# Cached values fetched page by page by SP, GpSimd's splits moved, x kept by samples, half of it and the tokens stored later

## The reference

```
x = x + L0(x)   # gated MLP, 1376 wide: down(silu(gate(x)) * up(x)), each with adapters
x = x + L1(x)   # linear 512 -> 512 with bias and adapters
x = x + L2(x)   # the same, other weights
x = x + L3(x)   # attention over a paged cache
# L3, per sample: 32 query heads and 8 key heads of size 128, page size 32, 16 pages
q, k, v = x @ Wq.T, x @ Wk.T, x @ Wv.T
q, k = rope(rmsnorm(q, wq), pos), rope(rmsnorm(k, wk), pos)   # pos = seqlen + arange(128)
k_all, v_all = concat(k_cache[block_table], k), concat(v_cache[block_table], v)  # 512 cached + 128 new
scores = q @ k_all.T / sqrt(128); cached keys at or past seqlen are masked with -1e30
o = softmax(scores) @ v_all;  L3(x) = o @ Wo.T
```

## Time and profile before

| | |
|---|---|
| median of 3 runs | 1463.56 us |
| profiled execution | 1464.6 us |
| its span | 1462.9 us |
| TensorE busy | 1371.6 us, 94% of the span |
| VectorE, ScalarE, GpSimd busy | 77%, 57%, 43% |

### The profile page before, as it was taken

The page is one execution under the profiler, slowest core; times in us unless marked ns, Lnnn a source line. Parts: engine busy times, 40 slices in busy tenths (PEclk is TensorE's granted clock), DMA queues, the critical chain, the costliest instruction groups (busy, mean ns, idle before and its releaser), DMA issues.

```text
span 1462.9 us, 26792 instructions
## 1 busy us (share of the span) xinstructions
PE 1371.6 (94%) x7308; PEld 1161.9 (79%) x7308; DVE 1127.4 (77%) x2945; ACT 838.2 (57%) x1951; POOL 631.5 (43%) x726
## 2 busy tenths in 40 slices
PE   6999999937999999789999998899999989999996
PEld 5888888726888888678888887788888877888885
DVE  5532446738888889788888888788888888888885
ACT  5632333237555667565666676566666765665564
POOL 4000000027444446674445468545554685444441
PEclk9999999968999999999999999999999999999999
DMA  8111300193322243332222443222224332222211
GB/s 303 50 58 44 108 24 26 63 328 86 78 62 59 57 115 88 93 79 59 57 57 57 122 107 86 58 64 66 66 63 120 96 95 64 65 74 61 57 30 14
DMA packets 127314, 119.30 MB, mean 82 GB/s; under 512 B 84128, under 2 KB 94752, under 8 KB 127008
## 3 DMA queue, kind: packets, MB, share of 16 engines
q0 software_dynamic: 19936, 57.69, 15.2%
q1 hardware_dynamic: 106608, 60.51, 14.6%
q10 hardware_dynamic: 720, 0.54, 0.1%
HBM read 101.90 MB, written 16.78 MB: 81 GB/s over the span
## 4 chain that ended last, share of the span: by engine, by line
PE 60%; DVE 7%; issue 6%; POOL 3%; ACT 2%; DMA 1%; DVEq 0%; POOLq 0%; ACTq 0%
PE bank L1335 14%; PE tail L1374 13%; PE wide L1404 12%; PE tail L1451 11%; PE wide L1369 6%; PE bank L1356 3%; POOL wqT L1201 2%; DVE ra L1655 1%; DVE prT L1664 1%; DVE ra L1659 1%; DVE rb L1656 1%; ACT pr L1525 1%; DMA rope<-rope_tables 1%; PE tail L1426 1%; POOL wkvT L1201 1%
## 5 line engine op out<-in xcount | busy, mean ns | idle before, releaser
L1525 ACT ACTIVATE pr<-pr,nm,q_scale 128x640 f32<-128x640 f32 x256 | 235.7, 921 | 111.7 <-DVE nm L1689 110.5
L1374 PE MATMUL tail<-prT,vt 128*128 128x512 f32 x960 | 259.9, 412 | 24.3 <-DVE prT L1664 24.3
L1166 POOL TENSOR_TENSOR tick<-tick 128x1 f32<-128x1 f32 x191 | 58.9, 308 | 419.6 <-PE wide L1404 345.6
L1374 PEld LDWEIGHTS tail<-prT,vt 128*128 128x128 f32 x960 | 174.3, 193 | 67.5 <-DVE prT L1664 35.1
L1685 DVE CUSTOM_DVE_ANT_0 pr<-wide,bias 128x640 f32<-128x640 f32 x256 | 209.8, 819 | 14.4 <-issue 14.2
L1335 PE MATMUL bank<-wqT,xTb 128*128 128x512 f32 x768 | 206.3, 397 | 1.3 <-POOL wqT L1201 1.3
L1451 PE MATMUL tail<-woT,oT 128*128 128x512 f32 x768 | 195.9, 398 | 0.0
L1664 DVE TENSOR_TENSOR prT<-wide,prT 128x1024 fp32r<-128x1024 f32 x128 | 153.5, 1220 | 24.4 <-ACT prT L1517 22.3
L1404 PE MATMUL wide<-kT,qT 128*128 128x320 f32 x512 | 162.7, 318 | 7.7 <-DVE mx L1685 7.7
L1451 PEld LDWEIGHTS tail<-woT,oT 128*128 128x128 f32 x768 | 139.6, 188 | 26.8
L1404 PE MATMUL wide<-kT_low,qT 128*128 128x320 f32 x512 | 158.6, 310 | 0.0
(11 more groups left out here) (239 smaller groups left out, 2669.3 us busy)
## 6 DMA issues: line engine op xcount, KB each, us to landing
w_ring<-pair_weights SPq DMA_DIRECT2D x80, 256.0 KB, 3.6
xTb<-x_transposed POOLq DMA_DIRECT2D x32, 512.0 KB, 3.9
k_raw<-k_pages SPq DMA_DIRECT2D x512, 32.0 KB, 1.8
rope<-rope_tables POOLq DMA_DIRECT2D x32, 256.0 KB
out<-y POOLq DMA_DIRECT2D x32, 256.0 KB, 4.1
w_raw<-w_gate_up SPq DMA_DIRECT2D x10, 512.0 KB, 3.2
x_transposed<-xh SPq DMA_DIRECT2D x8, 512.0 KB, 6.5
w_raw<-w_down SPq DMA_DIRECT2D x11, 256.0 KB, 2.9
```

Of the source, the lines that this page charges most:

```text
L1166: nc.gpsimd.tensor_tensor(tick[:, 2:3], tick[:, 1:2], tick[:, 1:2], ALU.add).then_inc(s_carry, 1)
L1374: last = nc.tensor.matmul(tail[g][:, :], vt[:, v_part, j, g * D:(g + 1) * D], prT[:, p_part, j, :], start=(j == 0 and v_part + p_part == 0 ...
L1525: ac.activation(pr[:, h, :], pr[:, h, :], ACT.Exp, bias=nm[:, h:h + 1], scale=q_scale[:, 0, head(h)], accum_out=den[:, h:h + 1]).then_inc( ...
```

## The change

- The values are laid out in DRAM by page and pair, and SP loads them with 16 DMAs per unit as it does the keys. The row numbers, their making in the first block and the four gathers are gone. SP also loads the rope table of each unit, once the unit before has been rotated.
- GpSimd's key split waits in addition for the first six normalisations of the unit before; its value split for both rotations and for the sums of the unit before, no longer for the first score. `add_share` comes after the value split and adds the share of the unit just before.
- In the last unit of a pair GpSimd makes chunks 0 to 2 before the value split and 3 to 11 after it (before 0 to 7 and 8 to 11), from VectorE's third step on. In the first unit it makes all eight output chunks after the value split (before four and four). ScalarE's copies stand earlier to match.
- `mask_keys` stands first in VectorE's turn.
- `xh` is laid out by sample, so that a sample is one run of 4096 bytes per partition. The first block stores only samples 0 to 3 of it. Samples 4 to 7 and the tokens are stored by GpSimd in the attention block, whose first action is the load of the first x. SP now waits in the first block until its four stores have landed.
- SP's order at the start of attention: 8 weight chunks, rope, 4 chunks, keys, values, 4 chunks (before: 12 chunks, keys, 4 chunks).
- The tensors in SBUF are placed in another order, so that what is still being stored isn't overwritten.

The diff, cut to its core:

```diff
@@ first block, SP @@
-                for c in range(2):
-                    sp.wait_ge(s_xl, 2 * 2 * KT + (c + 1) * KT)
-                    for i in range(c * BLK, (c + 1) * BLK):
-                        sp.dma_start(x_scratch[i].rearrange("p (t c) -> p t c", t=2 * KT),
-                                     xh[:, :, :, i * S:(i + 1) * S].rearrange("p i k c -> p (i k) c").bitcast(F32)).then_inc(s_xs, 16)
-                    for i in range(c * BLK, (c + 1) * BLK):
-                        sp.wait_ge(m_free[i % 2], i // 2 + 1)
-                        sp.dma_start(out[i], x_tok[:, i, :]).then_inc(s_init, 16)
+                sp.wait_ge(s_xl, 5 * KT)
+                for i in range(BLK):
+                    sp.dma_start(x_scratch[i], flat(xh[:, i], "i k c").bitcast(F32)).then_inc(s_xs[0], 16)
                 sp.wait_ge(s_ropest, 16)
+                sp.wait_ge(s_xs[0], 16 * BLK)
...
@@ attention @@
-    EARLY = {"next": ((0, 1, 2, 3), (4, 5), (6,), (7,)), "out": ((), (12, 13), (14,), (15,)), None: ((), (), (), ())}
+    EARLY = {"next": ((0,), (1, 2, 3), (4, 5, 6, 7), (8,), (9,), (10,)), "out": ((), (), (), (12, 13), (14,), (15,)), None: ((),) * 6}
...
+            load_x(0)
...
+            for i in range(BLK, B):
+                nc.gpsimd.dma_start(x_scratch[i], xh[:, i].rearrange("p i k c -> p (i k c)").bitcast(F32)).then_inc(s_xs[1], 16)
...
+            def split_keys(u, n):
                 pool.wait_ge(s_k, u * (16 * NPP) + 16 * NPP)
                 pool.wait_ge(s_sfull, u * HP + HP)
+                pool.wait_ge(s_p[0], u * SOON + FIRST)
...
+            def split_values(u, n):
+                pool.wait_ge(s_vnew, u + 1)
+                pool.wait_ge(s_v, u * (16 * NPP) + 16 * NPP)
+                pool.wait_ge(s_pv, u * G + FIRST)
+                pool.wait_ge(s_rope, u * G + 2 + FIRST)
...
+            def turn(pair, b, n, share, then_x, stored, extra=None):
+                u = unit(pair, b)
+                split_keys(u, n)
                 if then_x is not None:
                     pool.wait_ge(s_q1, u + 1)
                     carry(n + 1)
                     load_x(then_x)
                     n = n + 1
+                if share is None:
+                    for i in range(B):
+                        nc.gpsimd.dma_start(out[i], x_tok[:, i, :]).then_inc(s_init, 16)
+                share_room(u, stored)
+                if extra == "next":
+                    pool.wait_ge(s_step, u * NSTEP + 3)
+                    low_weights(pair + 1, 0, 3)
+                split_values(u, n + 1)
+                if share is not None:
+                    add_share(u - 1, share, n + 2)
+                else:
+                    pool.wait_ge(s_init, 16 * B)
                 if extra:
+                    low_weights(chunk_pair(pair, extra), *((3, 3 * KT) if extra == "next" else (3 * KT, NCHUNK)))
...
+            def load_rope(pair, b):
+                sp.wait_ge(s_rope, unit(pair, b) * G + FIRST)
+                sp.dma_start(rope[:, :, :].rearrange("p i d -> p (i d)"),
+                             rope_scratch[bass.ds(b, 1)].rearrange("o p n -> (o p) n")).then_inc(s_ropel, 16)
+
+            def load_values(pair, b, pages):
+                sp.wait_ge(s_vs, unit(pair, b) + FIRST)
+                for j, page in enumerate(pages):
+                    i = j % (P // PSIZE)
+                    sp.dma_start(v_raw[i * PSIZE:(i + 1) * PSIZE, j // (P // PSIZE), :],
+                                 v_pages[bass.ds(page * NPAIR + pair, 1)].rearrange("o s n -> (o s) n")).then_inc(s_v, 16)
...
@@ SP, per pair @@
+                load_weights(pair, 4 * KT, NCHUNK)
+                load_unit(1, pair, 1)
                 with sp.Fori(0, B - 2) as b:
+                    load_unit(2, pair, b + 2)
                 load_weights(pair + 1, 0, 2 * KT)
+                pages = pages_of(3, 0)
+                load_weights(pair + 1, 2 * KT, 2 * KT + 3)
+                load_keys(pair + 1, 0, pages)
+                load_rope(pair + 1, 0)
+                load_weights(pair + 1, 2 * KT + 3, 4 * KT)
+                load_values(pair + 1, 0, pages)
...
@@ VectorE's turn @@
                 if front:
+                    mask_keys()
                     arrive()
                     v.tensor_copy(qk[:, 0:REP, :], bank[1][:, :].rearrange("p (h d) -> p h d", d=D)).then_inc(s_q0, 1)
```

More of the change, by code:

```diff
@@ L231, in build_program @@
         s_xl = sem("x_updated_low_part")
-        s_xs = sem("x_stored")
+        s_xs = [sem(f"x_stored{c}") for c in range(2)]
         s_tok = sem("x_tokens_ready")
@@ L386, in main @@
                         for w_part, x_part in PASSES:
-                            last = nc.tensor.matmul(gate_up_place(j, c, w), wT[:, j % 2, w, w_part, k, :], xh[:, x_part, k, half(c)],
+                            last = nc.tensor.matmul(gate_up_place(j, c, w), wT[:, j % 2, w, w_part, k, :], x_half(x_part, k, c),
                                                     start=(k == 0 and w_part + x_part == 0), stop=False)
@@ L399, in lora_a @@
                                 out = wide[c][:, (2 * w + q) * 2 * S:(2 * w + q + 1) * 2 * S]
-                                tokens = slice(pair * 2 * S, (pair + 1) * 2 * S)
+                                two = slice(2 * pair, 2 * pair + 2)
                                 a_part = a_hl[:, w * KT:(w + 1) * KT, pair].rearrange("p k t m -> p k (t m)")
@@ new lines, in _ @@
+            turn(0, 0, 0, None, 1, False, "out")
+            pool.wait_ge(s_xs[1], 16 * BLK)
+            turn(0, 1, 3, 0, 2, False)
+            BEGUN = 3 + CARRIES
+            with pool.Fori(0, NPAIR - 1) as pair:
+                with pool.Fori(0, B - 3) as b:
+                    turn(pair, b + 2, pair * NCARRY + b * CARRIES + BEGUN, b + 1, b + 3, True)
+                turn(pair, B - 1, pair * NCARRY + (BEGUN + CARRIES * (B - 3)), B - 2, 0, True, "next")
+                turn(pair + 1, 0, pair * NCARRY + (BEGUN + CARRIES * (B - 2)), B - 1, 1, True, "out")
+                turn(pair + 1, 1, pair * NCARRY + (BEGUN + CARRIES * (B - 1)), 0, 2, True)
@@ L1273, in _, with pages_of @@
+            turn(pair, B - 1, pair * NCARRY + (BEGUN + CARRIES * (B - 3)), B - 2, None, True)
+            pool.wait_ge(s_out, 16 * (NPAIR * B - 1))
+            nc.gpsimd.memset(tick[:, 3:4], 0.0).then_inc(s_added, 1)
+            add_share(NPAIR * B - 1, B - 1, pair * NCARRY + (BEGUN + CARRIES * (B - 2) - 1))
+            pool.wait_ge(s_out, 16 * (NPAIR * B))
         @block.sync
         def _(sp):
-            def load_keys(site, pair, b):
+            def pages_of(site, b):
                 held = [sp.alloc_register(f"page{site}_{j}") for j in range(NPP)]
-                sp.load(held, table[0:1, bass.ds(b, 1), :, :].rearrange("p b t g -> p (b t g)"))
-                pages = [sp.snap(r, donate=True, min_val=0, max_val=PAGES - 1) for r in held]
+                sp.load(held, table[0:1, bass.ds(b, 1), :].rearrange("p b j -> p (b j)"))
+                return [sp.snap(r, donate=True, min_val=0, max_val=PAGES - 1) for r in held]
@@ L1280, in load_keys @@
+            def load_keys(pair, b, pages):
                 sp.wait_ge(s_klo, unit(pair, b) + FIRST)
@@ L1564, in turn, with early @@
                     squares(0, REP + G, REP)
+                def early(place):
+                    for i in EARLY[extra][place]:
+                        if i == 0:
+                            act.wait_ge(c_full[0], before[0] + 1)
+                            act.wait_ge(c_full[1], before[1] + 1)
+                        high_weights(chunk_pair(pair, extra), i)
                 if back:
                     high_probs(1, 0)
+                    early(0)
                     high_probs(1, 1)
@@ L1571, in turn @@
                     copy_values(0)
+                early(1)
                 own = BACK[0] if back else 0
@@ L1604, in turn @@
                             new_keys_values(n + 1)
+                if not back:
+                    act.wait_ge(s_xs[1], 16 * BLK)
             for i in range(3 * KT):
@@ L1766, in _ @@
                 low_weights(0, i)
+            dve.wait_ge(s_keyno, 2)
             turns(dve, turn)
```

216 lines of the change are left out of this document (72 added, 144 removed).

## The result

The changed kernel is slower: 1487.32 us (median of 4 runs, 1485.61 to 1489.1) against 1463.3 us, a ratio of 1.0165 with a 95% interval of 1.0148 to 1.0183. I had forecast 1423 us. The profiled execution has a span of 1485.2 us, 22.3 more than before.

What follows compares the result with a forecast made beforehand. TensorE bounds ordinary units (33.52 us each); boundaries lose 41.3 us, and the step to attention loses more. Boundaries -32, first units -3, stores -6, mask and splits +1 sum to -40 us: 1423 us, range 1407 to 1440.

Steps and rivals of the forecast that it cites:

- Weights at a boundary: Where one key-head pair gives way to the next: chunks ready early, 3 us still lost per boundary, 32 us gained.
- rival 4: Ordinary units: GpSimd's subtraction goes ahead of the mask, TensorE waits 2.4 us in 28 units, 1490 us; chance 0.04.
- The key mask: Mask first in VectorE's turn: TensorE loses 0 to 0.5 us per unit; 1 us lost in all, splits included.
- rival 2: The mask takes part back: 0.5 us of TensorE in 28 units, +14 in place of +1, 1436 us; chance 0.14.
- Rope and values by SP: Each unit: SP issues rope and value pages early enough, 18.6 us of pages with keys; VectorE's 3.14 us wait goes.
- The start: Start of attention: 6 us gained from the stores of x, 3 us from the first units.
- the stores: Fewer stores of x ahead of the first block's end: attention starts 7.3 us earlier, 6 us gained, bounds 1 and 11.

## Why the prediction was wrong

**Weights at a boundary: the step that failed.** I wrote that VectorE's two-operand steps stay beside the chunks and took 3 us for each boundary, "or 20 if each boundary keeps 7" as the bound. The chunks up to 10 came early: they ended at 591.5, where I had counted on 594.7 for chunk 11. Chunk 11 itself was made from 595.94 to 597.38, because ScalarE was held up behind the normalisation; TensorE waited for no chunk. I priced each meeting of VectorE and GpSimd as one instruction beside one, by the 1.55 us beside 2.98 of the earlier trace rows, and took chunks made early as good in themselves. In the kernel before no row of chunks kept a normalisation for over 1.6 us. The change put the share's issue and eight released chunks behind one another, and one normalisation waited for the whole row, 9.65 us in one unit and 6.38 in the next. The term should have been +4.7 per boundary (14.1 over three), not -10.7. With the wait per chunk alone it is -8.3, -7.4 and -7.4 us (75.79, 72.45 and 70.98 against the intervals of before), -23 in all; with the old order in ordinary units as well it is -12.1, -7.9 and -7.8, -27.7 of the 32 that I had forecast. So most of the plan's gain was there, and the long normalisations took it and more.

The Trainium skill (SBUF — State Buffer, Who interferes with whom) has VectorE in a two-port mode and GpSimd exclude each other for a whole instruction, the first to start winning. No row says which mode a normalisation is in. The trace agrees for one against one: the 1.55 us normalisation ends 0.34 us behind the value subtraction that it met. Read as I read it, it bounds a wait by the one instruction that runs; the 9.65 us beside eight shows that it doesn't always. My rival 4 asked who goes next, which was the right question, at the wrong place.

**The key mask.** I had 0 to 0.5 us per unit and took 1 us in all; rival 2 had 0.5 per unit, +14. Measured 0.43 per unit. The duration was right (1.01 us median, "0.5 to 1.2"). What failed was the slack. I set it at 0.7 us per unit and so nearly the whole cost at nothing. The two waits ahead of the low parts, 0.35 and 0.40 us, are indeed gone, but they took only 0.5 of the 0.95 us by which the copy is late, and TensorE, which already waited 0.26 us per unit for the second low part, had no slack of its own there. I also didn't see that mask and value split are one edit.

**Rope and values by SP.** Right: SP issues the rope a unit ahead, no wait of VectorE for it is left, and 16 value pages took 7.3 to 7.4 us of issuing in most units where I had 9.3.

**The start.** I took 9 us (6 and 3) and measured 4.1 up to the first ordinary unit: 3.0 to the first marker and 1.2 in the first interval. The block did start early (300.9 against 306.3) and TensorE's first product at 306.91 against 317.72. It then went at the pace of the weights, and reached the transposes of the first rotation only 3.5 us earlier (331.89 against 335.39), after 5.11 us of wait where there had been 7.27. In a range of 1 to 11 for the stores that is a size, not a mechanism.

```profile
306.91 3.10 PE L1332 MATMUL bank<-wkvT,xTb 128*128 128x512 f32 x6 [9.15 <-DVE wkvT L1621]
...
331.89 1.54 PE L1353 MATMUL bank<-ident,ra 128*128 128x128 f32 x6 [5.11 <-DVE ra L1739]
```

**The end.** Not in the prediction at all: I read no row behind the last share. It costs 3.5 us.

## What to carry to other kernels

When an edit moves GpSimd's work, look at what then stands in a row. Subtractions without a gap directly behind an accumulating store kept VectorE's normalisation out until the row ended, up to 9.8 us; rows as long elsewhere didn't. A wait for the instruction before is enough to open such a row, for 0.16 us each. Where a row may be of the first kind, price the meeting by the length of the row and not of one instruction. Slack counts only if the engine that needs the result has some of its own.

## What the hardware showed that I had not expected

- A normalisation of 0.54 us lasted 9.65 us beside a row of eight gapless subtractions behind the share's issue, 6.38 beside the output chunks behind the next one, 3.6 where a gap came after three, and at most 1.7 with a gap after each. Each of the long ones ended 0.36 us behind the last subtraction.
- Beside gapless rows that stand elsewhere, of up to eight, no normalisation that began there lasted over 1.7 us.
- In the rows behind the share's issue the subtractions start every 1.2 to 1.3 us and last 1.5 to 1.6 by the trace, so each starts some 0.3 us before the one ahead ends. One with a gap took 1.27 to 1.68.
- GpSimd's closing drain took 6.27 to 6.41 us in every kernel made from the changed one and 1.62 to 1.76 in those made from the one before; a last ordinary instruction made no difference.
